# An eleven-stage audio tower on one core: next stage's constants and rows issued earlier, router means kept on the chip, a norm's power one gap sooner, and shared activation tables at the tokenizer's end

## The reference

```python
# tokenizer: spectra of windows, a soft mask, a soft minimum
M = abs(fft(kernels(windows)));  Mmax = max(M, axis=-1)
Mt = M * sigmoid(M - 0.12 * Mmax)
x = soft_minimum(Mt, 0.9 * Mmax)          # -logsumexp over the pair
# layer 0: x = x + attention(x), then a router over the mean token
logits = mean(x, axis=1) @ Wr + br        # [64, 8], one row for each batch row
p = softmax(logits); p = softmax(p * scale(loads)); top 2 of 8 experts
x = layer_norm(x + sum_k w_k * expert_k(x))
# layer 1: retention, then a block with two norms
xg = x * rstd(x) * ln1_w                  # RMS norm ahead of causal attention
h = x + causal_attention(rope(xg @ wq), rope(xg @ wk), xg @ wv) @ wo
x = h + experts(norm(h))                  # dense pass over the experts
# layers 2 and 3: attention, gated or routed feed-forward
```

## Time and profile before

| what | value |
|---|---|
| median of 3 runs | 4176.56 us (4174.68 to 4178.3) |
| the profiled execution | 4173.4 us |
| its span | 4171.6 us, mean granted clock 0.926 |
| PE busy | 3724.6 us, 89% |
| DVE busy | 2822.9 us, 68% |
| ACT busy | 2307.4 us, 55% |
| POOL busy | 1969.3 us, 47% |

### The profile page before, as it was taken

One profiled execution on the slowest core, in us unless ns is written; L12 is line 12 of the kernel. 1 busy time (PEld: TensorE's weight loads), 2 busy tenths in 40 slices (PEclk: granted clock), 3 DMA queues, 4 the chain that ended last, 5 costly groups with the idle time before them and its releaser, 6 DMA issues.

```text
span 4171.6 us, 110110 instructions
## 1 busy us (share of the span) xinstructions
PE 3724.6 (89%) x31697; PEld 2593.0 (62%) x31697; DVE 2822.9 (68%) x9352; ACT 2307.4 (55%) x5677; POOL 1969.3 (47%) x2276
## 2 busy tenths in 40 slices
PE   7499947697999889999898769999999999899999
PEld 7366624485666656666687546666666666555555
DVE  2488849685888744444465778888888887455554
ACT  5455525322444434444343547888888888455555
POOL 0144438674565422222375655566556655343433
PEclk9999977797999999999855879999999999899999
DMA  2111124331111233333111220000000001333332
GB/s 54 35 34 34 33 44 114 85 83 37 36 39 37 61 75 77 79 81 81 45 39 40 64 66 10 12 12 12 14 13 12 12 12 29 78 72 78 72 80 57
DMA packets 465512, 203.02 MB, mean 49 GB/s; under 512 B 435090, under 2 KB 455566, under 8 KB 465170
## 3 DMA queue, kind: packets, MB, share of 16 engines
q1 hardware_dynamic: 465298, 200.65, 21.3%
HBM read 154.67 MB, written 45.91 MB: 48 GB/s over the span
## 4 chain that ended last, share of the span: by engine, by line
PE 73%; DVE 10%; issue 6%; POOL 5%; SPq 2%; DMA 2%; ACT 1%; DVEq 0%; POOLq 0%; ACTq 0%
PE att_pS L3694 6%; PE att_pP L3707 6%; PE att_pO L3726 5%; PE sw_pH L4208 5%; PE moe_pH L2744 5%; PE sw_pY L4195 5%; PE moe_pY L2767 4%; PE moe_pH L2748 3%; PE att_pS L983 2%; DVE att_M L1193 2%; PE moe_pH L2754 2%; PE att_pQ L3667 2%; PE att_pS L2237 1%; PE att_pO L1045 1%; PE ret_pR L1854 1%
## 5 line engine op out<-in xcount | busy, mean ns | idle before, releaser
L3593 POOL TENSOR_TENSOR att_P<-att_P,att_rden 125x498 f32<-125x498 f32 x512 | 509.6, 1016 | 384.9 <-DVE att_rden L3899 384.9
L3790 ACT ACTIVATE att_P<-att_Z,att_nb 125x249 f32<-125x249 f32 x1024 | 499.3, 493 | 10.5 <-DVE att_nb L3911 10.5
L2809 DVE TENSOR_TENSOR moe_hT<-moe_silu,moe_pH 128x498 f32<-128x498 f32 x384 | 258.8, 674 | 310.9 <-ACT moe_silu L2793 310.9
L3911 DVE CUSTOM_DVE_ANT_0 att_Z<-att_pS,att_mask 125x249 f32<-125x249 f32 x1024 | 380.4, 409 | 104.6 <-PE att_pS L3694 87.8
L4256 ACT ACTIVATE sw_hT<-sw_pH,sw_b 128x498 f32<-128x498 f32 x512 | 317.9, 672 | 220.1 <-PE sw_pH L4208 220.1
L2793 ACT ACTIVATE moe_silu<-moe_pH 128x498 f32<-128x498 f32 x384 | 225.1, 586 | 261.8 <-PE moe_pH L2748 176.0
L2720 POOL TENSOR_TENSOR moe_xe<-moe_share,moe_x 128x1992 f32<-128x1992 f32 x32 | 130.0, 4064 | 428.4 <-DMA moe_share<-mixing 392.1
L4115 POOL TENSOR_TENSOR sw_acc<-sw_acc,sw_Z 128x249 f32<-128x249 f32 x224 | 154.0, 688 | 364.2 <-DVE sw_Z L4335 363.4
L3797 ACT ACTIVATE att_PTr<-att_pP 125x996 f32<-125x996 f32 x256 | 255.8, 999 | 123.9 <-PE att_pP L3707 116.9
L3694 PE MATMUL att_pS<-att_kT,att_qT 64*125 64x249 f32 x2048 | 284.7, 396 | 25.9 <-DVE att_nb L3911 25.7
L3707 PEld LDWEIGHTS att_pP<-att_ident,att_P 124*125 124x125 f32 (+1 forms) x2048 | 244.3, 189 | 88.6 <-issue 88.6
(11 more groups left out here) (463 smaller groups left out, 9636.0 us busy)
## 6 DMA issues: line engine op xcount, KB each, us to landing
moe_share<-mixing SPq DMA_DIRECT2D x64, 498.0 KB
sw_share<-mixing SPq DMA_DIRECT2D x64, 498.0 KB, 5.6
ffn_W<-in_ffn_pairs SPq DMA_DIRECT2D x64, 192.0 KB, 2.4
att_F<-h_stream SPq DMA_DIRECT2D x192, 62.5 KB
att_X<-h_stream SPq DMA_DIRECT2D x192, 62.5 KB
h_stream<-att_H SPq DMA_DIRECT2D x64, 62.5 KB
ffn_F<-h_stream SPq DMA_DIRECT2D x64, 62.5 KB
ret_F<-h_stream SPq DMA_DIRECT2D x64, 62.5 KB
```

What stands on the lines that cost most here:

```text
L2809: v.tensor_tensor(hT[:, u, k, :, :], sl[:, k % 3, :, :], pH[:, k % 3, :, T:2 * T], ALU.mult).then_inc(*hid_ready.one())
L3593: g.tensor_tensor(own, own, bc(rden[:, j % 2, c, :], T), ALU.mult).then_inc(*scaled.one())
L3790: ins = a.activation(P[:, r, c, t, :], Z[:, r, c, t, :], ACT.Exp, scale=-1.0, bias=nb[:, r, c, t:t + 1], accum_out=den[:, r, c, t:t + 1])
L3911: ins = v.tensor_tensor_reduce(Z[:, s % 2, c, t, :], pS[:, c, t * T:(t + 1) * T], mask[:, u, s // HP, t, :], -1.0, -TAKEN, ALU.add, ALU.mi ...
```

## The change

Four things are edited.

1. **The weave of stages on SP.** A stage now yields three times instead of twice before its body: begin and constants | first rows | body. The last two pairs but two (28 and 29) are taken out of the loops into a piece of their own (`nearly`). In `joined` the next stage's begin and constants come ahead of store(28), keep(30), store(29), keep(31) of the stage before, and its first rows behind them.
2. **The router's means.** The tile `mean` is kept in SBUF and read by the router's matmuls. The two stores, the load and their waits are gone. The logits are now made by four matmuls instead of one: for each parity of the batch rows one over 64 channels, and one with a single row of ones for the bias. The router's batch order becomes parity first, and the three places where it is copied out are permuted accordingly.
3. **The causal attention's norm.** `norm.spread` goes from step 4 to 3 on DVE, `norm.power` from step 5 to 4 on POOL.
4. **The tokenizer.** From step 3 on, chunks 1 and 2 are in the same slots, and abs, exp and ln go through both chunks before the next function.

```diff
@@ joined @@
     for stage in stages:
         next(stage)
         next(last, None)
         next(stage)
+        next(last, None)
+        next(stage)
         last = stage
-    next(last, None)
+    for _ in range(2):
+        next(last, None)
@@ streamed, and a new function @@
-    for n in range(2 * whole, PAIRS - 2):
+    for n in range(2 * whole, PAIRS - 4):
         if n + lead < PAIRS:
             ahead(sp, n + lead, (n + lead) % 2)
+        store(sp, n, n % 2)
+        keep(sp, n + 2, n % 2)
+
+
+def nearly(sp, keep, store):
+
+    for n in (PAIRS - 4, PAIRS - 3):
         store(sp, n, n % 2)
         keep(sp, n + 2, n % 2)
@@ retention, SP (six other stages in the same manner) @@
             const(sp, cl, decay[:, :], A["const_decay"])
+
+        yield
+
+        @block.sync
+        def _(sp):
             sp.wait_ge(*before["stored"].after(0, 0))
             sp.wait_ge(*before["stored"].after(1, 1))
             opened(sp, ahead, keep)
@@ first feed-forward, SP @@
-            for i in range(30, PAIRS + 3):
+            for i in range(30, PAIRS + 1):
                 slot(sp, i, i % PERIOD)
...
+        @block.sync
+        def _(sp):
+            for i in range(PAIRS + 1, PAIRS + 3):
+                slot(sp, i, i % PERIOD)
@@ causal attention, SP, a new piece @@
+            for n in (PAIRS - 4, PAIRS - 3):
+                store(sp, n, n % 2)
+                keep(sp, n + 2, n % 2)
+                store_mix(sp, n - 2, n % 2)
@@ experts, SP @@
-            with sp.Fori(0, PAIRS // 2 - 1) as j:
+            with sp.Fori(0, PAIRS // 2 - 2) as j:
...
+            for n in (PAIRS - 4, PAIRS - 3):
+                load_x(sp, n + 2, n % 2)
+                store(sp, n, n % 2)
+                load_h(sp, n + 2, n % 2)
@@ first attention, end on SP @@
             closed(sp, store, stored)
             sp.wait_ge(*mean_ready.after(PAIRS - 1))
-            for b in range(2):
-                dst = mean_dram[:, b:b + 1]
-                sp.dma_start(bass.AP(dst.tensor, dst.offset, [[BATCH, C], [2, PAIRS]]),
-                             mean[b * C:(b + 1) * C, :].rearrange("c (n k) -> c n k", k=2)[:, :, b],
-                             allow_slow_non_contiguous=True).then_inc(*mean_stored.one())
-            sp.wait_ge(*mean_stored.after(0))
@@ router @@
-            const(sp, const_loaded, mT[0:C, :], mean_dram[:, :])
...
-            pe.matmul(pL[:, 0, :], mT[:, :], wr[:, :], start=True, stop=True).then_inc(*logits.one())
+            for b in range(2):
+                r, at = slice(b * C, (b + 1) * C), slice(b * PAIRS, (b + 1) * PAIRS)
+                pe.matmul(pL[at, 0, :], mean[r, :].rearrange("c (n k) -> c n k", k=2)[:, :, b], wr[r, :], start=True,
+                          stop=False)
+                ins = pe.matmul(pL[at, 0, :], ones[0:1, 0:PAIRS], br[:, :], start=False, stop=True)
+            ins.then_inc(*logits.one())
@@ causal attention, POOL @@
+                if step == 4:
+                    norm.power(g, n)
                 if step == 5:
-                    norm.power(g, n)
                     g.wait_ge(*xT_done.before(n))
@@ causal attention, DVE @@
-                if step == 4:
+                if step == 3:
                     norm.spread(v, n, 1e-5, (1.0 + 1e-6, 1e-11))
@@ tokenizer @@
-            return [c for c, (lo, hi) in enumerate(CHUNKS) if hi + step == s]
+            return [c for c, (lo, hi) in enumerate(CHUNKS) if (hi if step < 3 or c == 0 else GROUPS - 1) + step == s]
@@ tokenizer, ACT @@
                     a.activation(lg[:, q, :], lg[:, q, :], ACT.Abs).then_inc(*gap_abs.one())
+                for c in chunk_at(s, 5):
+                    q = pairs(c)
                     a.wait_ge(*gap_abs.after(c))
                     a.activation(lg[:, q, :], lg[:, q, :], ACT.Exp, scale=-1.0).then_inc(*gap_exp.one())
+                for c in chunk_at(s, 5):
+                    q = pairs(c)
                     a.wait_ge(*gap_exp.after(c))
                     a.activation(lg[:, q, :], lg[:, q, :], ACT.Ln, bias=bias[:, 3:4]).then_inc(*gap_log.one())
```

More of the change, by code:

```diff
@@ L1954, in _ @@
         def _(sp):
+            nearly(sp, keep, store)
+        yield
+        @block.sync
+        def _(sp):
             closed(sp, store, stored)
@@ L2101, in _ @@
                     store_mix(sp, n - 2, u)
-            for n in range(PAIRS - 6, PAIRS - 2):
+            for n in range(PAIRS - 6, PAIRS - 4):
                 store(sp, n, n % 2)
```

75 lines of the change are left out of this document (53 added, 22 removed).

## The result

The changed kernel takes 4115.74 us in the median of four runs (4112.78 to 4116.98), the kernel before 4175.62 (4170.78 to 4178.3, four runs). The ratio is 0.9857, with a 95% interval of 0.984 to 0.9874, so the kernel is 1.4% faster, by 59.9 us. The prediction was 4101, a gain of 75.8 us, with a range of 4084 to 4124. The direction and the range held; about 16 of the forecast 76 us did not come.

The account below looks back on a forecast made before the run. PE was taken as the bound (73% of the chain's span), so gains come where it idles. The terms sum to -75.8 us, taking the median from 4176.56 to about 4101, range 4084 to 4124.

Parts of the forecast that it names:

- The router: Between first attention and router: the means' stores and the load behind them go, logits become four matmuls; -21.0 us.
- The tokenizer: Tokenizer's end: three table loads fall away, but chunk 1 leaves later and the first store's start decides; +3.3 us.
- The border into retention: First feed-forward to retention: SP's list of first rows, up to F2, comes earlier; -6.5 us.
- the loop of the causal attention: Causal attention's pairs: POOL's power starts 0.64 us earlier, PE gains 0.62 in each of about 28 pairs; -17 us.
- the border into the experts: Causal attention to experts: constants sooner, so the queue drains about 13 us earlier and the mixing tile is freed; -12.5 us.
- The next limit is POOL: it was free at 1458.85: Step at the border into the experts: POOL needs 4.05 us for the first gated rows, to 1462.9; PE had started at 1475.57.
- the border into the causal attention: Retention to causal attention: F0 comes 5.4 us earlier, 1.2 of it lost to late last H; -4.2 us.
- the two borders of the depth-gated stage: Into it, F2 issued at 2283.0 to 2283.5 against 2296.57, -13.0 us; out of it, to third attention, -5.4 us.
- the border into the third attention: Depth-gated stage to third attention: DVE's 5.75 us idle for the last constant goes, keep(30) later costs up to 0.5; -5.4 us.
- In the experts the late row: Experts to windowed attention: constants and semaphore work now stand ahead of the load that POOL waits for; +0.5 us.
- The prediction's own sign of being wrong, a last H over 3 us late behind the block: At a stage's end: the forecast is wrong if the last H is over 3 us late behind the block.
- The second rival (the block hits the pairs that are left): At the borders: X(30) and X(31) come late, so the borders give half of their 41.6 us; 4122 us, chance 0.12.

Follow-up runs that it names:

- Two attempts to place the block better, later and earlier: Changed kernel, constants block between keep(30) and store(29), or three pairs ahead of the stage's end, into causal and third attention: medians 4119.57 and 4119.27 us.
- the last kernel above: Changed kernel with tokenizer undone, GpSimd's first experts product behind the last mixing weights, old order into router and windowed attention: median 4106.45 us, ratio 0.9838.

## Why the prediction was right, and where 16 us went

**Right by its own steps.** The router came out at -21.1 for -21.0, and the run with it alone shows that nothing takes it up again. The tokenizer came out at +3.2 for +3.3: the first store, not the last table, decides. Three table loads of 1.28 us less on ACT made the kernel slower. (Not every change of function costs a load: the listing ahead of the prediction has none ahead of abs.) This is also the answer to the Trainium skill's rule on grouping by table set (ScalarE: Activation LUTs, "Rules for kernel authors"): it holds for ACT's own time, and the stage is not bound by it. The border into retention gave 5.8 for 6.5.

**Right in its mechanism, with a part that was not forecast: the loop of the causal attention.** It gave 16.3 for 17, but a pair is shorter by 0.51 instead of 0.62 us. The sum took 0.93 us of waits from the one pair of the earlier trace rows; over 23 pairs of the kernel before the two waits are 0.82 us a pair, and 0.20 is left of them, the new wait for the maxima included. What made up for part of it was not forecast. In the kernel before, PE's granted clock had risen to its higher level 27.0 us behind the stage's first product, fell back to 0.50 from 1007.6 to 1014.4 and rose again, and the two powers on either side are 16.42 us apart. In the changed kernel it rose once, 31.3 us behind the first product, and stayed, and no pair from there on takes over 13.9 us. With the norm undone the fall is back (6.8 us, and 16.30 us between two powers), and it is there with the router alone. In the 9 us ahead of the fall in the kernel before PE was idle for 1.8 us, 0.9 of them waiting for POOL's `att_xg`, the wait that the edit removes. Why the clock fell there is not shown beyond that.

**Wrong: the border into the experts.** The step that failed is "The next limit is POOL: it was free at 1458.85". This took POOL's product as something that only needs POOL. It started the moment POOL was free, as forecast, and held VectorE for 7.1 us in the middle of the last mixing weights, on which PE waits. The term was -12.5, and -6.1 was measured. With POOL's product held back 3.6 us came back. The other 2 to 3 us are ACT's wait for the stores that free a mixing tile, which the sum took to be over before POOL's product ends and which still ends the border in that run.

**Mis-sized: late rows behind the block.** For the border into the causal attention the prediction had the last two H late by 1.1 to 1.4 us; they were late by 2.9 and 3.7. The block's length was right, but two things were missing. The first X issues behind the constants are slow themselves (1.83 and 3.99 us for two issues, against 0.97), and VectorE's wait of 4.01 us held back the next pair's product as well. -1.8 came for -4.2. Of the 18.4 us at the two borders of the depth-gated stage 3.3 are missing, and they are missing at its end: the first product of its last pair came 13.3 us earlier against the end of the windowed attention, for a forecast of 13.0 (its pairs wander by 1 to 2 us), but the border into the third attention gave 1.8 for 5.4, since the last H was 3.4 us late behind the row of pair 30. In the experts the late row cost 1.3 for 0.5. The prediction's own sign of being wrong, a last H over 3 us late behind the block, has come at both these borders, so this part of its mechanism was wrong in size, and the total held because the other terms are so much larger. The second rival (the block hits the pairs that are left) had this mechanism; it would have cost 21 us, and the pieces here are about 8. Two attempts to place the block better, later and earlier, gave nothing at either border. In them placing it moved the delay from one pair to another and did not absorb it.

**Not foreseen, and small.** The experts' first pair lost 1.3 us. PE's granted clock is its lower level there, 0.50 (1.2 of 2.4 GHz), until 1434.1, which is 5.8 us from the stage's first product. Windows of the changed kernel (the last three numbers are PE's granted clock, the DMA share and GB/s):

```profile
1432.00:1434.00 2.00, 2.00 (x12) 1.77 (x12) 0.67 (x1) 0.89 (x2) 0.00 (x0) 0.50 0.00 0
1434.00:1436.00 2.00, 2.00 (x22) 1.95 (x20) 1.25 (x2) 1.23 (x3) 0.00 (x0) 0.98 0.00 0
```

PE makes 12 products in 2 us at the one level and 22 at the other. In the kernel before the rise came 3.0 us from the stage's first product, and in the last kernel above 3.3. Over all twelve kernels the later the rise, the longer the first pair, in the same order throughout: from 24.96 us (first product to ACT's output of pair 0) with the rise at 3.0 to 26.40 with the rise at 6.1. So the clock is the cause of the 1.3 us. Why it rose late is open: no single edit goes with it, since the kernel with the router alone had 4.8 and the last kernel, with the weave, 3.3. The last 1.7 us look like chance as well: from the first product of the third attention to that of the switch stage the kernel before took 1086.0 us, the changed one 1088.1, and the others between 1084.5 and 1089.7, though nothing is changed there.

## What to carry to other kernels

Constants for the next stage are not free because their queue waits anyway: what they delay is the first transfer behind them, and on engines in order that delay travels to the stage's end. Before an operation of a second engine is set loose earlier, look at what is running beside it at that time, above all between VectorE and GpSimd, and let the one on the critical path go first. And fewer instructions on an engine (here three table loads) are worth nothing where they put off the transfer that ends the stage. Last, read a wait that a sum rests on over many pairs and not from one.

## What the runs showed of the hardware

A VectorE instruction with two inputs in SBUF that starts during a GpSimd product of 4.1 us waits for the rest of it: 4.25 us instead of 0.42, and 3.47 instead of 0.19. Such time shows as VectorE's busy time in the profile, not as idle time with a releaser, so the waits don't name it; only the length of one instruction against its neighbours does. It is not so for every GpSimd instruction: in the first feed-forward of the changed kernel VectorE's sum `ffn_H` (125x256, both inputs in SBUF) ran 30 times wholly inside a GpSimd power of 1.02 us (125x4) and took its usual 0.41 to 0.42 us each time. The two DMA issues of an X row took 0.97 us on SP's queue in the last pairs of both stages of the kernel before. Behind the five constants of the third attention they took 3.8 to 4.8 us in all nine kernels with the weave, and behind the eleven of the causal attention only 1.8 to 2.2, so the number of constants does not decide it; what does is not shown. And PE's granted clock rose from 0.50 to 1.00 between 3.0 and 6.1 us behind the experts' first product in the twelve kernels, with the same products in the same order.
